# Where convolution inputs, third sums and a third split stand in four hand-written orders

## The chip, the cores and the metric

The kernel runs on one core of one Trainium2 chip. The metric is the device time of one execution in microseconds (us). Besides its five engines the core has 16 DMA engines; SP issues most transfers, ACT issues the gate tables.

## The reference, cut to what matters

Two layers follow one another, both on x of shape 32 x 64 x 1024. A layer has a convolution-like step and a feed-forward step whose result is added to x:

```python
# layer 0
y = conv1d(x, weight, taps=9, groups=4) + cond @ c_weight.T + bias       # 64 channels
x = x + y @ W.T + b + lora(y)                                            # W: 1024 x 1024, rank 16
# layer 1
mix_w, mix_b = softmax(mlp(cond)) @ (8 matrices, 8 biases)               # per sample
v = mix_w[sample] @ x + mix_b[sample]                                    # 64 x 64 over channels
scores = v @ Wr.T;  gates = softmax over the top 16 of 64 experts
h = v @ A.T          # 64 experts x rank 16 = 1024 columns
x = x + 2 * ((h * gates spread over 16 columns each) @ B)
```

All is f32. The kernel splits every operand of the large products in two parts, a high one (rounded to the matmul's type fp32r) and the rest as a low one, and makes three matmuls of each: high by high, high by low, low by high.

## The kernel before, in words

The 32 samples run as four groups of eight (512 tokens, four tiles of 128). Each group does, on PE: the convolution (`conv`, eight samples, banks shared with the end of the group before), the first product with W, the mixing (`mix`, eight column chunks), scores and h = v A (`h_of`, eight pieces), and the last product with B. Weights come in *pieces* of 128 x 1024. A raw piece lands in one of two (in the first group three) raw buffers, ACT writes its high part (`split_raw` or `split_first` on ACT), DVE its low part (the same names on DVE). The first group (`first_group` of every engine) uses 24 raw pieces plainly, piece 16 to 23 for the last product. The groups 1 to 3 (`group`) have 36 steps and use Strassen-Winograd for the two large products, seven half-size products instead of eight; a piece then takes 12 matmuls of 128 x 512 and not 24. The combined weights for that are made once: four *units* of four matrices are loaded (`load_weights`), summed on DVE (`combine`: four instructions), split (`combined_hi` on ACT, `combined_lo` on DVE) and written to DRAM (`keep_weights` on SP), from where later groups fetch them (`fetch`). Units 0, 1 and 2 fall in the first group, unit 3 in group 1. Units 1 to 3 use the buffer `conv_in` as their place of work, so that the next group's convolution inputs (`load_conv_in`, four loads of 516 KB) can only follow them.

Every engine's order is written out by hand, and only semaphores tie the engines. What the rest speaks of:

- SP's queue is in order: an instruction that waits holds up all that is behind it. `next_raw(n)` waits until DVE has made the low part of the piece two raw loads before (`lo_done`), then loads a raw piece. `next_x` waits until a tile pair of x has been stored and loads the next group's. `cond_bias` and `mix_bias` load bias tables of 256 KB.
- In the first group DVE multiplies h by the gates chunk by chunk (`gated`, `gated_lo`) and has `combine(2)` after chunk 5. The last product's piece 19 needs chunks 6 and 7 and `split_first(19)`.
- At the end of the first group DVE adds four half tiles (`add(banks[4 + t]...)`, then `dve.sem_inc(s_o, 8)`) to x. The convolution of group 1 takes those banks from its third sample on (`pe.wait_ge(s_o, g * 22 - 8)`). Just before these adds DVE makes the low parts of three raw pieces of group 1, `split_raw(0, STEPS + 0, 1, 2)`; SP loads the third of them by `next_raw(26)`.
- The gates go from `gate` through PE (transposed), ACT (`gates_out`) and DRAM to `gate_x`: eight loads of 256 KB (`spread_gates`), four after ACT's split of piece 20, four more as the buffers come free. DVE's `gated(g, c)` waits for the c-th. The last product needs all eight chunks from piece 24 on; after chunk 7 DVE makes four sums (`sums(4)`, L1162 to L1167) and then the low part of piece 25.

The lines that are printed below are those of the profile.

Of the kernel before, what the change touches and what calls it, by code (L numbers as in the profile page):

```python
# [69 lines left out]
def adaln_ffn_kernel(nc, conv_x, x, taps, pieces, first_consts, hidden_w, later_consts, lora_a, lora_b,  # L70
                     starts, wr, expand, spread, out):
    with ExitStack() as ctx:
# [240 lines left out]
        def _(sp):  # L313
# [82 lines left out]
            def first_group():  # L396
# [61 lines left out]
                load_conv_in(1, 3)  # L458
                for t in range(NT):
                    store(0, t, 0, t + 1)  # L460
                next_x(0, 0, 0)
                next_x(0, 1, 0)
                next_raw(26)
                next_raw(27)
                for t in range(NT):
                    store(0, t, 1, 11 + t)
                next_x(0, 0, 1)
# [4 lines left out]
            def group(g, last):  # L472
# [21 lines left out]
                next_raw(16)  # L494
                next_raw(17)
                if g == 1:
                    keep_weights(3, 0)
                    keep_weights(3, 1)
                next_raw(18)
                next_raw(19)  # L500
                if g == 1:
                    keep_weights(3, 2)
                    keep_weights(3, 3)
                for n in range(20, 24):
                    next_raw(n)
                    if not last:
                        load_conv_in(g + 1, n - 20)
                if not last:
                    cond_bias(g)
                    mix_bias(g)  # L510
                if g == 1:
                    for i in range(4):
                        sp.wait_ge(s_comb[i], 32 * 4)
# [111 lines left out]
        def _(act):  # L625
# [184 lines left out]
            def group(g, last):  # L810
                def next_split(n):

                    step_used(act, g, n - SLOTS)
                    split_raw(g, n)

                for b in range(GB):
                    conv_hi(g, b)
                    if b == 1:

                        act.wait_ge(s_conv, g * GB + 1)  # L820
                        split_raw(g, 3)
                first_product(g, 0, (4, 5))
                sums_hi(g, 0)
                lora_parts(g)
                next_split(8)
                next_split(9)
                next_split(14)
                next_split(15)
                for i, c in enumerate(CHUNKS):
                    split_hi(g, MIX0 + i, v_hi[:, c, :], work[:, c, :])  # L830
                if g == 1:
                    combined_hi(3, 0)
                    combined_hi(3, 1)
                score_out(g, 5)
                if g == 1:
                    combined_hi(3, 2)
                    combined_hi(3, 3)
                next_split(16)
                gates_exp(g)
                next_split(17)  # L840
                next_split(18)
                gates_out(g, 0)
                next_split(19)
                next_split(20)
                act.wait_ge(s_gates_out, 16 * g + 16)
                for c in range(GATES):
                    spread_gates(c)
                next_split(21)
                for c in range(NCH):
                    if g == 1 and c % 2 == 0:  # L850
                        act.wait_ge(s_comb[c // 2], 32 * 4)
                    gated_hi(g, c)
                    if c == 1:
                        next_split(22)
                    if c == 3:
                        next_split(23)
                    if c == 6:
                        next_split(24)
                next_split(25)
                first_product(g, 1, (6, 7))  # L860
                sums_hi(g, 4)
                next_split(32)
                next_split(33)
                if not last:
                    next_split(STEPS)
                    next_split(STEPS + 1)
                    next_split(STEPS + 2)
# [6 lines left out]
        def _(dve):  # L874
# [128 lines left out]
            def first_group():  # L1003
# [124 lines left out]
                for c in range(NCH):  # L1128
# [3 lines left out]
                    gated_lo(0, c)  # L1132
                    if c in (1, 3, 5):
                        split_first(16 + c // 2)
                    if c == 5:
                        combine(2)
                split_first(19)
                for step in range(4):
                    combined_lo(2, step)
                for n in range(20, 23):  # L1140
# [4 lines left out]
                dve.wait_ge(s_o, 4)  # L1145
                dve.sem_inc(s_o, 6)
                split_first(23)
                for n in range(3):
                    split_raw(0, STEPS + n)
                for t in range(NT):  # L1150
                    dve.wait_ge(s_fin, NT + t + 1)
                    add(banks[4 + t][:, :], t, 1, s_o)
                dve.wait_ge(s_o, 14)
                dve.sem_inc(s_o, 8)  # L1154
                for i in range(4):
                    dve.wait_ge(s_comb[i], 32 * 3)

            def group(g, last):
# [102 lines left out]
                for i, c in enumerate(CHUNKS):  # L1261
                    mix_item(g, i, c, (6, 7, 4)[i % 3])
                    if i:
                        mix_lo(g, i - 1, CHUNKS[i - 1])
                mix_lo(g, NCH - 1, CHUNKS[-1])
                if g == 1:
                    combined_lo(3, 0)
                    combined_lo(3, 1)
                split_raw(g, 16)
                choose(g, 1)  # L1270
                split_raw(g, 17)
                if g == 1:
                    combined_lo(3, 2)
                split_raw(g, 18)
                if g == 1:
                    combined_lo(3, 3)
                for n in range(19, 22):
                    split_raw(g, n)
                dve.wait_ge(s_lo, g * ITEMS + H0)
                for c in range(0, 6, 2):  # L1280
# [496 lines left out]
```

## Time and profile before

| | us |
|---|---|
| median of 3 runs | 690.73 |
| lowest, highest | 690.48, 694.65 |
| the profiled execution | 691.47 |
| its span, first to last instruction | 689.7 |
| PE busy in it | 659.3 (96%) |
| DVE, ACT, POOL busy | 453.2 (66%), 212.8 (31%), 74.4 (11%) |
| mean granted TensorE clock | 0.985 of full |
| traffic | 157.98 MB, 229 GB/s |

The profiled execution's time is 1.8 us more than its span. PE works nearly all the time, and matmuls are pipelined, so its busy share alone does not tell what can be had: one has to look at the places where it stands still and at the clock that it is granted. In a timeline row the bracket is the idle time of that engine before the instruction and what ended it. A row whose line is in a helper (L1355 to L1357 are the three matmuls of every product, L881 every `split_raw` of DVE, L887 every `split_lo`) has to be told apart by its time and its tiles.

### The profile page before, as it was taken

The numbers are of one execution on the slowest core, as the hardware profiler recorded it, in microseconds if no ns is written. First come the engines' busy times: TensorE is split into PE (matmuls) and PEld (weight loads), VectorE is DVE, ScalarE is ACT, GpSimd is POOL, SyncE is SP. The second block draws the span as 40 slices with busy tenths as digits, with TensorE's granted clock in tenths as the row PEclk, the third lists the DMA queues.
The fourth block names the chain that finished last, engine by engine and source line by source line (L and its number), as shares of the span: only waits on it lengthen the run. The fifth ranks groups of instructions, "written<-read, shape, count | busy, mean of one in ns | idle before, by whom it ended". The sixth has DMA issues, their size and how long they took to land.

```text
span 689.7 us, 8350 instructions
## 1 busy us (share of the span) xinstructions
PE 659.3 (96%) x3197; PEld 543.7 (79%) x3197; DVE 453.2 (66%) x688; ACT 212.8 (31%) x275; POOL 74.4 (11%) x91
## 2 busy tenths in 40 slices
PE   9999999989969999996999999999799999999997
PEld 8878888867868788875779788888588878888775
DVE  2869568557168786746768749644866965665864
ACT  2723234314133215224223402422513521243510
POOL 1699000000000070000000025000000000000000
PEclk9999999999989999998999999999999999999999
DMA  8568517948846852697785771077797666037585
GB/s 303 220 242 330 219 47 224 344 141 333 312 149 244 333 195 85 242 309 263 275 319 212 304 297 68 30 231 226 250 338 272 229 260 241 30 99 210 214 329 190
DMA packets 51450, 157.98 MB, mean 229 GB/s; under 512 B 5472, under 2 KB 6368, under 8 KB 51424
## 3 DMA queue, kind: packets, MB, share of 16 engines
q1 hardware_dynamic: 46096, 148.05, 59.4%
q10 hardware_dynamic: 5328, 9.61, 4.6%
q8 instruction: 13, 0.21, 0.1%
q14 instruction: 13, 0.11, 0.0%
HBM read 131.94 MB, written 25.71 MB: 229 GB/s over the span
## 4 chain that ended last, share of the span: by engine, by line
PE 43%; DMA 14%; DVE 8%; issue 3%; ACT 2%; SPq 1%; DVEq 0%; ACTq 0%
PE bank L1355 10%; PE bank L1357 10%; PE bank L1356 10%; DMA gate_x<-gates 7%; PE bank L1369 6%; DMA raw<-pieces 3%; DMA piece_lo<-kept 3%; PE bank L1389 3%; DVE piece_lo L881 2%; ACT piece_hi L634 1%; DVE work L976 1%; PE bank L1376 1%; DVE x L913 1%; PE bank L1395 1%; PE bank L1396 1%
## 5 line engine op out<-in xcount | busy, mean ns | idle before, releaser
L881 DVE TENSOR_TENSOR piece_lo<-raw,piece_hi 128x1024 fp32r<-128x1024 f32 x60 | 74.2, 1239 | 97.0 <-ACT piece_hi L634 97.0
L1355 PE MATMUL bank<-piece_hi,u_hi 128*128 128x512 f32 x272 | 110.8, 407 | 15.3 <-DVE u_lo L887 8.8
L634 ACT ACTIVATE piece_hi<-raw 128x1024 fp32r<-128x1024 f32 x60 | 63.2, 1056 | 161.0 <-PE bank L1357 109.0
L1357 PE MATMUL bank<-piece_hi,u_lo 128*128 128x512 f32 x272 | 109.9, 404 | 0.0
L1356 PE MATMUL bank<-piece_lo,u_hi 128*128 128x512 f32 x272 | 109.8, 404 | 0.0
L1355 PE MATMUL bank<-v_hi,piece_hi 128*128 128x512 f32 x256 | 101.9, 398 | 0.1
L1357 PE MATMUL bank<-v_hi,piece_lo 128*128 128x512 f32 x256 | 101.1, 395 | 0.0
L1356 PE MATMUL bank<-v_lo,piece_hi 128*128 128x512 f32 x256 | 101.0, 394 | 0.0
L1355 PEld LDWEIGHTS bank<-piece_hi,u_hi 128*128 128x128 f32 x272 | 52.5, 193 | 31.4 <-issue 10.6
L1355 PE MATMUL bank<-piece_hi,v_hi 128*128 128x512 f32 x192 | 76.2, 397 | 0.4 <-DMA piece_lo<-kept 0.3
L1357 PE MATMUL bank<-piece_hi,v_lo 128*128 128x512 f32 x192 | 75.8, 395 | 0.0
L1356 PE MATMUL bank<-piece_lo,v_hi 128*128 128x512 f32 x192 | 75.7, 395 | 0.0
L639 ACT ACTIVATE u_hi<-work 128x512 fp32r<-128x512 f32 x64 | 40.2, 631 | 112.9 <-DVE work L976 70.1
L1369 PE MATMUL bank<-toep,conv_in 128*128 128x128 f32 x512 | 61.9, 283 | 6.9 <-DVEq L1154 6.9
L1369 PEld LDWEIGHTS bank<-toep,conv_in 128*128 128x128 f32 x512 | 60.8, 199 | 7.7 <-DVEq L1154 7.1
L913 DVE TENSOR_TENSOR x<-x,bank 128x512 f32<-128x512 f32 x82 | 51.9, 680 | 19.1 <-PE bank L1383 12.7
L1357 PEld LDWEIGHTS bank<-piece_hi,u_lo 128*128 128x128 f32 x272 | 52.6, 193 | 12.5
L1356 PEld LDWEIGHTS bank<-piece_lo,u_hi 128*128 128x128 f32 x272 | 52.6, 194 | 11.9
L1355 PEld LDWEIGHTS bank<-v_hi,piece_hi 128*128 128x128 f32 x256 | 48.1, 188 | 11.6 <-DVE work L976 0.6
L1357 PEld LDWEIGHTS bank<-v_hi,piece_lo 128*128 128x128 f32 x256 | 48.1, 188 | 11.6
L1356 PEld LDWEIGHTS bank<-v_lo,piece_hi 128*128 128x128 f32 x256 | 48.2, 188 | 11.0
L887 DVE TENSOR_TENSOR u_lo<-work,u_hi 128x512 fp32r<-128x512 f32 x64 | 43.8, 687 | 15.1 <-ACT u_hi L639 13.5
(143 smaller groups left out, 802.8 us busy)
## 6 DMA issues: line engine op xcount, KB each, us to landing
raw<-pieces SPq DMA_DIRECT2D x76, 512.0 KB, 5.3
piece_hi<-kept SPq DMA_DIRECT2D x48, 512.0 KB, 4.7
piece_lo<-kept SPq DMA_DIRECT2D x48, 512.0 KB, 5.7
conv_in<-conv_x SPq DMA_DIRECT2D x16, 516.0 KB, 7.9
x<-x SPq DMA_DIRECT2D x16, 512.0 KB, 5.2
gate_x<-gates ACTq DMA_DIRECT2D x32, 256.0 KB
out<-x SPq DMA_DIRECT2D x32, 256.0 KB, 2.5
conv_in<-pieces SPq DMA_DIRECT2D x12, 512.0 KB, 8.3
```

The costliest lines, as they stand in the source:

```text
L634: act.activation(piece_hi[:, n % SLOTS, :], raw[:, r % RAWS, :], ACT.Copy).then_inc(s_piece_hi, 1)
L639: act.activation(to, of, ACT.Copy).then_inc(s_hi, 1)
L881: dve.tensor_tensor(piece_lo[:, n % SLOTS, :], raw[:, r % RAWS, :], piece_hi[:, n % SLOTS, :].bitcast(F32), ALU.subtract).then_inc(s_piece ...
L887: dve.tensor_tensor(to, of, hi, ALU.subtract).then_inc(s_lo, 1)
L913: dve.tensor_tensor(half, half, of, ALU.add).then_inc(done, 1)
L976: dve.tensor_tensor(work[:, c, :], banks[bank][:, :], gate_x[:, c % GATES, :], ALU.mult).then_inc(s_item, 1)
L1355: pe.matmul(to, left_hi, right_hi, start=first, stop=False)
L1356: pe.matmul(to, left_hi, right_lo, start=False, stop=False)
L1357: return pe.matmul(to, left_lo, right_hi, start=False, stop=last)
L1369: mm = pe.matmul(banks[bank][:, cg * P:(cg + 1) * P], conv_in[:, b, cg, h:h + Q], toep[:, cg, 1 - h, :], start=(h == 0), stop=(h == 1))
L1376: mm = pe.matmul(banks[bank][0:LORA_M, :], lora_a_r[:, k, :], part[:, k, :], start=(k == 0 and part is u_hi), stop=(k == NCH - 1 and part ...
L1389: mm = pe.matmul(banks[bank][:, t * P:(t + 1) * P], x1[:, t, c * P:(c + 1) * P], blockdiag[:, t, :], start=True, stop=True)
```

## The change

It only reorders; no operation is added or removed.

- SP, first group: `next_raw(26)` stands ahead of both `next_x`, `next_raw(27)` between them.
- SP, groups 1 to 3: the four `load_conv_in` of the next group no longer alternate with raw pieces 20 to 23. In group 2 two of them stand between raw pieces 17 and 18 and two behind 18; in group 1 all four stand behind 18, and all four `keep_weights(3, ...)` between 17 and 18. `cond_bias` and `mix_bias` stand ahead of raw pieces 22 and 23 and not behind them.
- ACT and DVE, group 1: the four `combined_hi(3, ...)` and `combined_lo(3, ...)` stand inside the mix loop, one for every two chunks, and not behind it and behind the choice of experts.
- DVE, first group: `combine(2)` stands behind `split_first(19)`; `split_raw(0, STEPS + 2)` behind the four adds to x.

```diff
--- before.py
+++ after.py
@@ -458,10 +458,10 @@
                 load_conv_in(1, 3)
                 for t in range(NT):
                     store(0, t, 0, t + 1)
+                next_raw(26)
                 next_x(0, 0, 0)
+                next_raw(27)
                 next_x(0, 1, 0)
-                next_raw(26)
-                next_raw(27)
                 for t in range(NT):
                     store(0, t, 1, 11 + t)
                 next_x(0, 0, 1)
@@ -494,20 +494,25 @@
                 next_raw(16)
                 next_raw(17)
                 if g == 1:
-                    keep_weights(3, 0)
-                    keep_weights(3, 1)
+                    for step in range(4):
+                        keep_weights(3, step)
+                elif not last:
+                    load_conv_in(g + 1, 0)
+                    load_conv_in(g + 1, 1)
                 next_raw(18)
-                next_raw(19)
                 if g == 1:
-                    keep_weights(3, 2)
-                    keep_weights(3, 3)
-                for n in range(20, 24):
+                    load_conv_in(g + 1, 0)
+                    load_conv_in(g + 1, 1)
+                if not last:
+                    load_conv_in(g + 1, 2)
+                    load_conv_in(g + 1, 3)
+                for n in range(19, 22):
                     next_raw(n)
-                    if not last:
-                        load_conv_in(g + 1, n - 20)
                 if not last:
                     cond_bias(g)
                     mix_bias(g)
+                next_raw(22)
+                next_raw(23)
                 if g == 1:
                     for i in range(4):
                         sp.wait_ge(s_comb[i], 32 * 4)
@@ -828,13 +833,9 @@
                 next_split(15)
                 for i, c in enumerate(CHUNKS):
                     split_hi(g, MIX0 + i, v_hi[:, c, :], work[:, c, :])
-                if g == 1:
-                    combined_hi(3, 0)
-                    combined_hi(3, 1)
+                    if g == 1 and i % 2 == 0:
+                        combined_hi(3, i // 2)
                 score_out(g, 5)
-                if g == 1:
-                    combined_hi(3, 2)
-                    combined_hi(3, 3)
                 next_split(16)
                 gates_exp(g)
                 next_split(17)
@@ -1132,9 +1133,8 @@
                     gated_lo(0, c)
                     if c in (1, 3, 5):
                         split_first(16 + c // 2)
-                    if c == 5:
-                        combine(2)
                 split_first(19)
+                combine(2)
                 for step in range(4):
                     combined_lo(2, step)
                 for n in range(20, 23):
@@ -1145,13 +1145,14 @@
                 dve.wait_ge(s_o, 4)
                 dve.sem_inc(s_o, 6)
                 split_first(23)
-                for n in range(3):
-                    split_raw(0, STEPS + n)
+                split_raw(0, STEPS)
+                split_raw(0, STEPS + 1)
                 for t in range(NT):
                     dve.wait_ge(s_fin, NT + t + 1)
                     add(banks[4 + t][:, :], t, 1, s_o)
                 dve.wait_ge(s_o, 14)
                 dve.sem_inc(s_o, 8)
+                split_raw(0, STEPS + 2)
                 for i in range(4):
                     dve.wait_ge(s_comb[i], 32 * 3)
 
@@ -1262,19 +1263,12 @@
                     mix_item(g, i, c, (6, 7, 4)[i % 3])
                     if i:
                         mix_lo(g, i - 1, CHUNKS[i - 1])
+                    if g == 1 and i % 2:
+                        combined_lo(3, i // 2)
                 mix_lo(g, NCH - 1, CHUNKS[-1])
-                if g == 1:
-                    combined_lo(3, 0)
-                    combined_lo(3, 1)
                 split_raw(g, 16)
                 choose(g, 1)
-                split_raw(g, 17)
-                if g == 1:
-                    combined_lo(3, 2)
-                split_raw(g, 18)
-                if g == 1:
-                    combined_lo(3, 3)
-                for n in range(19, 22):
+                for n in range(17, 22):
                     split_raw(g, n)
                 dve.wait_ge(s_lo, g * ITEMS + H0)
                 for c in range(0, 6, 2):
```

## Rows read from the trace of the kernel before

**Rows 1.** The page, part 1: busy time, share and count of each engine.

```profile
PE 659.3 (96%) x3197; PEld 543.7 (79%) x3197; DVE 453.2 (66%) x688; ACT 212.8 (31%) x275; POOL 74.4 (11%) x91
```

**Rows 2.** The waits of PE: who for whom, us in total, times, longest.

```profile
PE bank L1355 <- DVE u_lo L887: 8.8, 3, 3.6
...
PE bank L1355 <- DVE piece_lo L881: 2.8, 2, 1.5
```

**Rows 3.** Timeline of PE: start, us, instruction [idle before it <- releaser].

```profile
155.99 0.50 PE L1355 MATMUL bank<-piece_hi,u_hi 128*128 128x512 f32 x1 [3.50 <-DVE piece_lo L1053]
...
196.20 13.35 PE L1369 MATMUL bank<-toep,conv_in 128*128 128x128 f32 x96 [6.94 <-DVEq L1154]
...
316.03 0.49 PE L1355 MATMUL bank<-piece_hi,u_hi 128*128 128x512 f32 x1 [2.20 <-DVE u_lo L887]
...
326.44 0.49 PE L1355 MATMUL bank<-piece_hi,u_hi 128*128 128x512 f32 x1 [3.02 <-DVE u_lo L887]
...
332.41 0.51 PE L1355 MATMUL bank<-piece_hi,u_hi 128*128 128x512 f32 x1 [1.38 <-DVE piece_lo L881]
...
490.14 0.49 PE L1355 MATMUL bank<-piece_hi,u_hi 128*128 128x512 f32 x1 [3.61 <-DVE u_lo L887]
...
496.12 0.50 PE L1355 MATMUL bank<-piece_hi,u_hi 128*128 128x512 f32 x1 [1.47 <-DVE piece_lo L881]
```

**Rows 4.** Stretches: us, busy (count) per engine, clock, DMA share, GB/s.

```profile
156.80:160.20 3.40, 3.40 (x10) 2.63 (x9) 3.40 (x4) 3.40 (x4) 0.00 (x0) 0.50 0.95 353
194.40:201.20 6.80, 5.00 (x23) 5.00 (x24) 5.39 (x8) 2.10 (x3) 0.00 (x0) 0.50 0.82 269
332.40:486.00 153.60, 153.58 (x763) 128.00 (x764) 101.11 (x163) 42.77 (x57) 13.47 (x17) 1.00 0.63 221
```

**Rows 5.** The chain of work: start, us, a group's convolution undisturbed.

```profile
363.54 14.29 PE bank L1369 x128
```

**Rows 6.** Timeline of DVE before the first group's piece 20.

```profile
145.47 1.23 DVE L987 TENSOR_TENSOR conv_in<-conv_in 128x1024 f32<-128x1024 f32 x1 [6.26 <-DMA conv_in<-pieces]
...
154.71 1.23 DVE L1053 TENSOR_TENSOR piece_lo<-raw,piece_hi 128x1024 fp32r<-128x1024 f32 x1 [0.25 <-ACT piece_hi L741]
...
160.40 1.22 DVE L1053 TENSOR_TENSOR piece_lo<-partial,piece_hi 128x1024 fp32r<-128x1024 f32 x1
```

**Rows 7.** Timelines of SP, then DVE, around the group's end.

```profile
182.18 1.67 SPq L324 DMA_DIRECT2D x<-x  x2
183.90 0.94 SPq L315 DMA_DIRECT2D raw<-pieces  x2
...
192.53 1.23 DVE L881 TENSOR_TENSOR piece_lo<-raw,piece_hi 128x1024 fp32r<-128x1024 f32 x1 [12.09 <-ACT piece_hi L634]
193.68 2.47 DVE L913 TENSOR_TENSOR x<-x,bank 128x512 f32<-128x512 f32 x4
```

**Rows 8.** Stretches from first gate load's issue to last one's landing.

```profile
296.50:322.30 25.80, 23.45 (x93) 18.32 (x92) 13.52 (x18) 8.84 (x12) 0.00 (x0) 0.93 0.84 274
458.80:485.90 27.10, 27.10 (x118) 21.96 (x117) 13.01 (x18) 7.70 (x11) 0.00 (x0) 1.00 0.84 249
619.80:643.90 24.10, 24.10 (x105) 19.36 (x104) 14.44 (x20) 9.02 (x12) 0.00 (x0) 1.00 0.69 196
```

**Rows 9.** Timeline of SP in group 1: raw 18 with 19, cond bias.

```profile
277.48 7.68 SPq L315 DMA_DIRECT2D raw<-pieces  x2
...
302.55 0.43 SPq L353 DMA_DIRECT2D cond_bc<-spread  x1
```

**Rows 10.** Timeline of PE in the last group, inside pieces 24 and 25.

```profile
652.50 0.40 PE L1357 MATMUL bank<-piece_hi,u_lo 128*128 128x512 f32 x1
653.00 0.50 PE L1355 MATMUL bank<-piece_hi,u_hi 128*128 128x512 f32 x1
```

**Rows 11.** Groups of DVE in group 1's mix loop: line, shapes, count, busy, mean.

```profile
L887 DVE TENSOR_TENSOR v_lo<-work,v_hi 128x512 fp32r<-128x512 f32 x8 | 5.5, 684 | 0.2
L920 DVE TENSOR_TENSOR work<-bank,mixb_bc 128x512 f32<-128x512 f32 x8 | 5.4, 686 | 2.4 <-PE bank L1389 2.3
```


## The prediction

> **What bounds the kernel now.** I read the page's busy shares first: PE is busy 659.3 of 689.7 us [rows 1]. So the time is PE's work plus the places where it stands still or runs at the lower clock, and a reordering can only take from those. The waits of PE name them in total [rows 2]: it waits for `u_lo` three times (8.8 us) and twice for `piece_lo` L881 (2.8 us). The timeline of PE gives each wait's place [rows 3]. There are seven of weight:
>
> - A, first group, before piece 19: 3.50 us.
> - B, group 1's convolution, before its third sample: 6.94 us, until DVE has passed the adds at L1154.
> - C, group 1, around the last product: 2.20, 3.02 and 1.38 us, 6.6 together.
> - D, group 2, same place: 3.61 and 1.47 us, 5.1 together.
>
> Then the granted clock. It is 1.00 (2.4 GHz) nearly everywhere, but 0.50 (1.2 GHz) for 3.4 us after wait A and for 6.8 us around wait B [rows 4]. The same happened after the waits of 2.20, 3.02 and 3.61 us, three more stretches like the first row of [rows 4]. After the wait of 1.38 us it stayed at 1.00 [rows 3, 4]. So a wait of 1.5 us costs only itself and one of 2.2 us costs 3.4/2 = 1.7 us more. For B: 96 convolution matmuls took 13.35 us [rows 3]; undisturbed, 128 take 14.29 us [rows 5], so 96 take 10.7, and the loss is 2.6 us.
>
> What can be had at most is A 3.5 + 1.7 = 5.2, B 6.9 + 2.6 = 9.5, C 6.6 + 2 x 1.7 = 10.0, D 5.1 + 1.7 = 6.8; together 31.5 us.
>
> **Part A: `combine(2)` behind the split of piece 19.** DVE stood 6.26 us until the four matrices of unit 2 had landed, at 145.47, and then needed four sums of about 1.2 us, 4.8 us, before it came to chunks 6 and 7. The low part of piece 19 began at 154.71, ended at 155.94, and PE started at 155.99 [rows 3, 6]. Now the chunks come first. Piece 19's raw load is the next in the queue behind those matrices: 512 KB at the 353 GB/s of [rows 4] is 1.5 us, so it lands at about 147; ACT's and DVE's parts take 1.1 and 1.2, and the piece is ready at about 149. PE wants it at 155.99 - 3.50 = 152.4: wait A goes. The stall moves to piece 20. A whole piece is 24 matmuls, at 24.1/105 = 0.23 us each [rows 8] 5.5 us, so PE wants piece 20 at 157.9. DVE has four sums (4.8), four `combined_lo` (155.94 to 160.40, 4.5) and the split (1.2) before it: 149.2 + 10.5 = 159.7 [rows 6]. A wait of 1.8 us is left. From below it is 0, from above 3.5; I take 1.8, without a fall of the clock, which lies between the 1.47 that had none and the 2.20 that had one (plus 1.7 if it falls). A gives 5.2 - 1.8 = 3.4 us. Behind piece 20 DVE needs 1.2 us a piece against PE's 5.5, so nothing more is late.
>
> **Part B: `next_raw(26)` early, its split behind the adds.** SP issued the two x loads at 182.18, when the output stores had landed, and raw 26 at 183.90. DVE's low part of it began at 192.53 after 12.09 us idle, and only then came the four adds (2.47 us) for which PE waited [rows 7]. Now the adds need only PE's own results: they are done about 1 us after PE's last product, and the first two samples of the convolution, 2 x 14.29/8 = 3.6 us [rows 5], cover that. Wait B goes with its clock loss, 9.5 us. What is queued behind on DVE is the split of raw 26 and then `conv_item(0)`, which PE's fifth sample needs, 7.1 us after the convolution's start. That start was 196.20 - 6.94 - 3.6 = 185.7 and is now 3.4 earlier, 182.3, so the item is wanted by 189.4. Raw 26 can be issued once the low part of raw 24 is made, and DVE's idle time shows that this was before 180.4; taking 179 and the 7.5 us that it took last time (183.90 to 192.53 less ACT's 1.1) [rows 7] it lands at 186.5, is split by 188.8, and the item is there at 189.5. So it is hidden, narrowly; from above it costs some 3 us. The x loads are read only after the whole convolution, over 14 us later, so moving two of them behind one raw load costs nothing; without that cover it would be 1.5 us each. ACT waits for raw 26 ahead of `conv_hi` as before.
>
> **Parts C and D: conv loads out of the gates' stretch.** When could the last product start? In group 1 at once, 316.03 - 2.20 = 313.8; in group 2 two pieces of 12 matmuls ahead of its wait, 490.14 - 3.61 - 24 x 0.23 = 481.0; in group 3 three ahead, 652.7 - 36 x 0.23 = 644.4 [rows 3, 10]. The first gate load was issued at 296.5, 458.8, 619.8 and the last landed 25.8, 27.1, 24.1 us later [rows 8]. So the gates left 17.3, 22.2 and 24.6 us ahead of the product, and group 3, which loads no convolution input and no bias, waits 0.3 us in all [rows 10]. With the conv loads gone (group 2) and the keep stores of unit 3 gone from between raw 18 and 20 (group 1), ACT gets raw 20 as early as in group 3, and the gates leave as early. What group 3 does not have are two bias loads, now ahead of raw 22 [rows 9]: 512 KB, 1.5 us at 353 GB/s. From below they cost 0 (the DMA engines of group 3's stretch are busy 0.69), from above what a gate load takes there, 2 x 24.1/8 = 6 us. I take 1.5: a wait of 0.3 + 1.5 = 1.8 us stays in each of both groups. D gives 6.8 - 1.8 = 5.0 us.
>
> The conv loads themselves go where the queue is quiet: 4 x 516 KB is 6 us. In group 1 they stand behind raw 18 and ahead of raw 19, whose issue waits for DVE's choice of experts: the two issues lay 7.68 us apart [rows 9], and that hides them. Without that cover, raw 19 would be late by up to 6 us.
>
> C has a cost of its own: four `combined_lo` of 1.2 us inside the mix loop. DVE's own work there is 5.5 + 5.4 us with 2.4 us of waiting for PE [rows 11]. So the 4.9 us added exceed the idle time by 2.5, the upper bound; the lower is 0. The last one stands directly ahead of the low part of chunk 7, which PE needs; I take that one, 1.2 us. Two of them previously stood behind the loop and ahead of piece 16, so nothing else grows. C gives 10.0 - 1.8 - 1.2 = 7.0 us.
>
> **Sum.** 3.4 + 9.5 + 7.0 + 5.0 = 24.9 us. The profiled execution took 691.5 us (span 689.7 and 1.8 around it), which gives 666.6; the median of the runs is 0.7 lower, which would give 665.8. I say 666.
>
> **A rule that speaks against it.** In group 3's stretch without conv loads, the gate loads are only 1.7 to 3.0 us faster, at a DMA share of 0.69 against 0.84 [rows 8]. The Trainium skill (DMA: Bandwidth & Descriptors, Queues, rings and completion order) says that each DMA engine takes turns between the queues that have work for it, packet by packet. By it the gates on ACT's queue gain nothing as long as SP's queue still has raw pieces; then C and D would yield only what the earlier start gives. This is the first rival.
>
> **The rivals.**
>
> 1. *The gates are no earlier.* Raw pieces and biases keep SP's queue full, the waits of C and D stay as they are, and the mix loop costs its 1.2. Gain 3.4 + 9.5 - 1.2 = 11.7: 679.8 us. For it: 1.7 to 3.0 us of [rows 8]. Against it: group 3 waits only 0.3 us. Chance 0.17.
> 2. *Raw 26 lands late anyway.* Its landing is behind the group's conv loads and stores, PE stands at its fifth sample, and B gives about 3 of 9.5: 673 us. Against it: 7 us of cover. Chance 0.08.
> 3. *The other side: the clock.* PE without pauses is granted less for long stretches. All of PE's some 650 us scale with it, so each hundredth costs 6.5 us; from a mean clock of about 0.95 on, the end is later than before, at 0.94 near 698 us. Against it: 1.00 over 153.6 us of unbroken work [rows 4]. Chance 0.03.
>
> **Chances and range.** The forecast has 0.72, its own range is 660 to 672: from nearly all 31.5 us gained to 1.7 of clock lost again at piece 20 and in groups 1 and 2. The range of 8 in 10 reaches to just short of rival 1, 659 to 678. A change of 1% (7 us) is about what a measurement can tell. Faster by over 1% holds for the forecast and for both first rivals: 0.94; within 1%, if two rivals meet: 0.04; slower: 0.02.
>
> **What would show it.** In the profile after: no idle time before piece 19 and under 2.2 us before piece 20; no wait at L1154; the gate loads issued some 24 us before the last product in all of groups 1 to 3; waits below 2 us there and no clock of 0.50 behind them; 1 to 2 us new idle time before L1395/L1396 in group 1. Wrong would be: gate loads that leave early and land as late as before (rival 1), or PE idle inside the convolution of group 1 (rival 2).

## The result and the profile after

| | before | after |
|---|---|---|
| median of the runs, us | 692.65 (4 runs) | 671.66 (4 runs) |
| lowest, highest | 690.48, 694.65 | 669.35, 672.66 |
| profiled execution, span | 691.47, 689.7 | 671.31, 669.5 |
| PE busy | 659.3 | 651.7 |
| mean granted clock | 0.985 | 0.996 |

The ratio is 0.9693, with a 95% interval of 0.9646 to 0.974: the changed kernel is 3.1% faster, some 21 us. The forecast was 666 in a range of 659 to 678. In three further sets of runs, below, the kernel before was at 690.6, 691.0 and 691.7, and the changed kernel, in the last of them, at 671.1.

The page of the kernel after, part 1, to be laid beside [rows 1]:

```profile
PE 651.7 (97%) x3197; PEld 538.4 (80%) x3197; DVE 451.1 (67%) x688; ACT 213.1 (32%) x275; POOL 73.2 (11%) x91
```

PE has 7.6 us less busy time though it has the same 3197 matmuls: that is the clock, not work. The waits of PE after (who for whom, us in total, times, longest), beside [rows 2]:

```profile
PE bank L1349 <- DVE piece_lo L882: 4.6, 3, 2.4
PE bank L1349 <- DVE piece_lo L1054: 3.4, 1, 3.4
PE bank L1349 <- DMA piece_lo<-kept: 1.3, 2, 0.9
```

The 8.8 us for `u_lo` are gone altogether. What is left at L1349 is for low parts of pieces. Where they are, the timeline of PE after shows (seven waits, beside those of [rows 3]; the second row is group 1's convolution, the fourth and fifth are in its mix loop):

```profile
161.79 0.50 PE L1349 MATMUL bank<-piece_hi,u_hi 128*128 128x512 f32 x1 [3.37 <-DVE piece_lo L1054]
...
185.77 14.46 PE L1363 MATMUL bank<-toep,conv_in 128*128 128x128 f32 x128
...
221.60 0.50 PE L1349 MATMUL bank<-piece_hi,v_hi 128*128 128x512 f32 x1 [0.94 <-DMA piece_lo<-kept]
...
251.76 0.47 PE L1389 MATMUL bank<-v_hi,wr_r 128*128 128x512 f32 x1 [0.25 <-DVE v_lo L888]
...
254.35 0.50 PE L1389 MATMUL bank<-v_hi,wr_r 128*128 128x512 f32 x1 [0.30 <-DVE v_lo L888]
...
315.29 0.50 PE L1349 MATMUL bank<-piece_hi,u_hi 128*128 128x512 f32 x1 [1.04 <-DVE piece_lo L882]
...
474.81 0.51 PE L1349 MATMUL bank<-piece_hi,u_hi 128*128 128x512 f32 x1 [2.40 <-DVE piece_lo L882]
...
632.77 0.50 PE L1349 MATMUL bank<-piece_hi,u_hi 128*128 128x512 f32 x1 [1.16 <-DVE piece_lo L882]
```

The convolution of group 1 is now one unbroken row of 128 matmuls, where [rows 3] had 6.94 us of waiting. The waits of 2.20 and 3.02 us in group 1 and of 3.61 in group 2 have no answering row; one wait before piece 25 remains in each of groups 1 to 3 (1.04, 2.40, 1.16 us). But the first group's wait did not go: it moved from 155.99 to 161.79 and is 3.37 us instead of 3.50. The clock and the DMA engines in five stretches after (us, busy and count per engine, clock, DMA share, GB/s), beside [rows 4] and [rows 8]:

```profile
162.60:165.90 3.30, 3.30 (x9) 2.62 (x8) 3.30 (x6) 0.00 (x0) 0.00 (x0) 0.50 0.77 169
475.00:480.00 5.00, 5.00 (x22) 4.06 (x22) 5.00 (x7) 0.66 (x1) 0.00 (x0) 1.00 0.81 302
281.10:305.10 24.00, 24.00 (x105) 19.30 (x104) 13.52 (x19) 8.25 (x12) 0.00 (x0) 1.00 0.68 219
439.40:464.30 24.90, 24.90 (x109) 20.20 (x108) 13.50 (x18) 7.72 (x11) 0.00 (x0) 1.00 0.66 210
598.50:623.80 25.30, 25.30 (x110) 20.33 (x110) 14.73 (x20) 8.84 (x12) 0.00 (x0) 1.00 0.69 187
```

The clock fell to 0.50 once, behind the wait of 3.37 us, and not behind the one of 2.40. The three lower rows run from the first gate load's issue to the last one's landing: 24.0, 24.9 and 25.3 us in groups 1 to 3, where it was 25.8, 27.1 and 24.1 before [rows 8]. So the gates travel only 1.8 and 2.2 us faster in groups 1 and 2, and 1.2 us slower in group 3, where nothing was edited. The rest is when they leave. ACT's first gate loads and PE's first matmul of the last product, in groups 1 and 2:

```profile
281.11 2.89 ACTq L691 DMA_DIRECT2D gate_x<-gates  x4
...
439.44 2.56 ACTq L691 DMA_DIRECT2D gate_x<-gates  x4
```

```profile
305.68 0.40 PE L1349 MATMUL bank<-piece_hi,u_hi 128*128 128x512 f32 x1
...
463.88 0.39 PE L1349 MATMUL bank<-piece_hi,u_hi 128*128 128x512 f32 x1
```

The gates leave 24.6 and 24.4 us ahead of the product, where they left 17.3 and 22.2 us ahead before; group 3 has 24.5, as it had. In group 1 the earlier issue, 7.3 us, is most of what changed; in group 2 it is half, 2.2 us.

### The profile page after: what moved, and what is told of

Read it like the earlier page. It is cut to its first block, busy times and chain, and to the rows that moved or that the text cites. A ratio compares the mean times of both kernels' runs of the same rounds, so it can differ in the third digit from the quotient of the medians.

```text
span 669.5 us, 8350 instructions
## 1 busy us (share of the span) xinstructions
PE 651.7 (97%) x3197; PEld 538.4 (80%) x3197; DVE 451.1 (67%) x688; ACT 213.1 (32%) x275; POOL 73.2 (11%) x91
## 4 chain that ended last, share of the span: by engine, by line
PE 59%; DMA 19%; DVE 14%; issue 3%; ACT 3%; ACTq 1%; SPq 0%; DVEq 0%
PE bank L1349 14%; PE bank L1351 13%; PE bank L1350 13%; DMA gate_x<-gates 12%; PE bank L1363 8%; DMA piece_lo<-kept 4%; PE bank L1383 3%; DMA raw<-pieces 3%; DVE piece_lo L882 2%; PE bank L1370 2%; ACT piece_hi L639 2%; DVE work L977 1%; DVE x L914 1%; DMA toep<-taps 1%; PE bank L1375 1%
## 5 line engine op out<-in xcount | busy, mean ns | idle before, releaser
L1349 PE MATMUL bank<-piece_hi,u_hi 128*128 128x512 f32 x272 | 109.0, 401 | 8.1 <-DVE piece_lo L882 4.6
L1350 PE MATMUL bank<-piece_lo,u_hi 128*128 128x512 f32 x272 | 107.9, 397 | 0.0
L1351 PE MATMUL bank<-piece_hi,u_lo 128*128 128x512 f32 x272 | 107.8, 396 | 0.0
L1349 PE MATMUL bank<-v_hi,piece_hi 128*128 128x512 f32 x256 | 101.8, 398 | 0.0
L1349 PE MATMUL bank<-piece_hi,v_hi 128*128 128x512 f32 x192 | 76.2, 397 | 1.3 <-DMA piece_lo<-kept 1.3
L1349 PEld LDWEIGHTS bank<-piece_hi,u_hi 128*128 128x128 f32 x272 | 51.5, 189 | 22.1 <-DVE piece_lo L882 5.9
L1363 PE MATMUL bank<-toep,conv_in 128*128 128x128 f32 x512 | 59.5, 276 | 0.7 <-DMA toep<-taps 0.6
L1363 PEld LDWEIGHTS bank<-toep,conv_in 128*128 128x128 f32 x512 | 58.3, 192 | 1.6 <-DMA toep<-taps 1.1
L1349 PEld LDWEIGHTS bank<-v_hi,piece_hi 128*128 128x128 f32 x256 | 48.1, 188 | 11.0
```

The lines of the kernel that those rows point to most:

```text
L1349: pe.matmul(to, left_hi, right_hi, start=first, stop=False)
L1350: pe.matmul(to, left_hi, right_lo, start=False, stop=False)
L1351: return pe.matmul(to, left_lo, right_hi, start=False, stop=last)
L1363: mm = pe.matmul(banks[bank][:, cg * P:(cg + 1) * P], conv_in[:, b, cg, h:h + Q], toep[:, cg, 1 - h, :], start=(h == 0), stop=(h == 1))
```

## Experiments: which part gave what

Each ratio is to the kernel before, timed in the same set of runs.

**Part A alone.** On DVE, to the kernel before:

```diff
-                    if c == 5:
-                        combine(2)
                 split_first(19)
+                combine(2)
```

> The kernel before with part A alone: combine(2) stands behind the split of piece 19, on DVE. Theory 1 (the wait only moves): PE stands 3 to 4 us before piece 20 and not before piece 19, the clock falls behind it as before, and the time is that of before within 1 us. Theory 2 (the forecast's step): the wait before piece 20 is 1.8 us without a fall of the clock, and the time is about 3.4 us less than before.

Measured: 691.42 against 690.61 us, ratio 1.0012 (0.9984 to 1.0040), 12 runs of it. PE's timeline, before piece 20, and the stretch behind it:

```profile
160.76 0.50 PE L1354 MATMUL bank<-piece_hi,u_hi 128*128 128x512 f32 x1 [1.77 <-DVE piece_lo L1053]
```

```profile
162.10:165.40 3.30, 3.30 (x10) 2.52 (x9) 3.26 (x5) 0.00 (x0) 0.00 (x0) 0.50 0.73 217
```

The wait has moved to piece 20, as both theories said. It was 1.77 us, the size that the forecast had (1.8), not theory 1's 3 to 4; but the clock fell behind it, which makes 3.5 us of it, where wait A cost 5.2. The time is theory 1's all the same: in this profile the waits of group 1 are 9.3 us with one fall of the clock, where they were 6.6 us with two before, and those of group 2 are 5.4 instead of 5.1, so most of the remaining 1.7 us was lost there. Whether the edit did that or the execution, this run does not tell.

**The changed kernel without part A.** The same diff the other way round, on the changed kernel.

> The changed kernel with part A undone: combine(2) again behind chunk 5. Theory 1: the wait stands before piece 19 again, as long as the one before piece 20 was, and the time is that of the changed kernel within 1 us (0.97 of before). Theory 2: 3.4 us more than the changed kernel (0.974).

Measured: 669.60 us, ratio 0.9681 (0.9645 to 0.9717); the changed kernel has 0.9693 and 0.9673, in other sets. Part A gives nothing that can be measured. PE's wait before piece 19, and the stretch behind it:

```profile
155.50 0.50 PE L1350 MATMUL bank<-piece_hi,u_hi 128*128 128x512 f32 x1 [2.44 <-DVE piece_lo L1054]
```

```profile
155.60:162.00 6.40, 6.40 (x28) 5.04 (x29) 6.40 (x6) 5.22 (x6) 0.00 (x0) 1.00 0.85 322
```

This wait is longer than the one in the run before it, and the clock stayed at 1.00. The old order was seen in six profiles, with waits of 3.50, 1.94, 2.45, 2.44, about 2.0 and 3.5 us before piece 19; the new one in five, with 3.37, 3.00, 1.77, 2.0 and 1.17 before piece 20. These are profiles of different kernels that share the order at this place. The wait differs by 1.6 us among the old ones and by 2.2 us among the new ones; the means are 2.6 and 2.3 us, the clock fell behind it in four of six and in three of five, and so the two orders lie over each other.

**Part B alone.** On SP and on DVE, to the kernel before:

```diff
+                next_raw(26)
                 next_x(0, 0, 0)
+                next_raw(27)
                 next_x(0, 1, 0)
-                next_raw(26)
-                next_raw(27)
...
-                for n in range(3):
-                    split_raw(0, STEPS + n)
+                split_raw(0, STEPS)
+                split_raw(0, STEPS + 1)
                 for t in range(NT):
                     dve.wait_ge(s_fin, NT + t + 1)
                     add(banks[4 + t][:, :], t, 1, s_o)
                 dve.wait_ge(s_o, 14)
                 dve.sem_inc(s_o, 8)
+                split_raw(0, STEPS + 2)
```

> The kernel before with part B alone: next_raw(26) ahead of the two x loads, and the third split behind the four adds. The forecast's step: the wait of 6.9 us inside group 1's convolution goes, and the clock loss of 2.6 us with it; 9.5 us less than before. If B only moves its wait to the fifth sample, 3 us less.

Measured: 681.86 us, ratio 0.9868 (0.9836 to 0.9899), 9.1 us of 690.6. The waits of PE in it:

```profile
PE bank L1356 <- DVE u_lo L887: 9.3, 3, 4.9
PE bank L1356 <- DVE work L976: 2.3, 1, 2.3
...
PE bank L1356 <- DVE piece_lo L881: 1.2, 2, 0.7
```

The wait at L1154 is gone and nothing stands in its place inside the convolution. The waits of groups 1 and 2 are not those of [rows 2]: 9.3 + 2.3 + 1.2 us in the first, second and last row instead of 8.8 + 2.8, 1.2 us more, about a tenth of the gain. That was given back there, or was a chance of this execution.

**Half of part B: DVE's order only.**

> The kernel before with half of part B: the third split behind the four adds, SP's order as before. Raw 26 then lands at about 191 as before, conv_item(0) comes at about 194, and PE, whose third sample is now free, stands before its fifth sample (wanted at about 193): 1 to 2 us instead of 6.9, so 7 to 8 us less than before. If SP's order was what mattered, under 3 us less.

Measured: 684.13 us, ratio 0.9908 (0.9873 to 0.9942), 6.4 us less than before. **The other half, SP's order only.**

> The kernel before with the other half of part B: raw 26 ahead of the x loads, DVE's order as before. Raw 26 lands at about 186, is split by 188.5, and the adds follow until 190.5, where PE wants its third sample at about 189.5: 1 to 2 us of waiting instead of 6.9, so 7 to 8 us less than before. If DVE's order was what mattered, under 3 us less.

Measured: 683.23 us, ratio 0.9894 (0.9864 to 0.9924), 7.3 us less. The rows of PE that started behind the wait, first with DVE's order, then with SP's:

```profile
193.12 0.71 PE L1370 MATMUL bank<-toep,conv_in 128*128 128x128 f32 x4 [3.29 <-DVE work L891]
```

```profile
190.96 0.49 PE L1369 MATMUL bank<-toep,conv_in 128*128 128x128 f32 x2 [1.72 <-DVEq L1154]
```

With DVE's order alone the wait is at the fifth sample and for `work` L891, `conv_item(0)`, which stands behind the split of a raw piece that landed at 190.1; it is 3.29 us where 1 to 2 were expected. With SP's alone it is at the third sample, for the adds, and 1.72 us. Either half takes most of the wait, since both shorten the same chain (stores, x loads, raw 26, its split, adds); in the profiles only both take all of it. The times alone do not tell a half from the whole: their intervals, 4.0 to 8.8 and 5.2 to 9.4 us, overlap that of part B (7.0 to 11.3). Both halves were expected to give 7 to 8 us, which lies in both. In the changed kernel the tail of that chain runs on DVE as follows (last add, split of raw 26, first item of the convolution):

```profile
185.97 0.69 DVE L914 TENSOR_TENSOR x<-x,bank 128x512 f32<-128x512 f32 x1 [0.71 <-PE bank L1351]
186.80 1.23 DVE L882 TENSOR_TENSOR piece_lo<-raw,piece_hi 128x1024 fp32r<-128x1024 f32 x1
187.94 0.68 DVE L892 TENSOR_TENSOR work<-bank,cond_bc 128x512 f32<-128x512 f32 x1
```

The item starts at 187.94, 2.2 us after the convolution, and is wanted after 7.1.

**Parts C and D alone.** The changed kernel with parts A and B undone as in the two diffs above.

> The kernel before with parts C and D alone (everything that the change does in groups 1 to 3). The forecast's step: 12.0 us less than before (7.0 in group 1, 5.0 in group 2). What the profile after shows at its waits makes it 8 to 13. The rival of the gates that are no earlier: 1 us more than before.

Measured: 681.28 us, ratio 0.9851 (0.9817 to 0.9885), 10.3 us less; 12.0 had been forecast, and the first rival's +1 is excluded. Its waits of PE:

```profile
PE bank L1363 <- DVEq L1155: 6.3, 1, 6.3
PE bank L1349 <- DVE piece_lo L882: 4.8, 3, 2.3
```

The first row is wait B, which this kernel keeps. The second holds the three waits before piece 25, 4.8 us together with nothing for `u_lo`. No run takes part C apart: the keep stores, the convolution loads and the four `combined_lo` moved together in group 1, so which of them lets the gates leave 7 us earlier there is not shown.

**The changed kernel without part D.** On SP; group 1 keeps its order, in group 2 the convolution loads alternate with raw pieces 20 to 23 again and the bias loads follow them:

```diff
                     for step in range(4):
                         keep_weights(3, step)
-                elif not last:
-                    load_conv_in(g + 1, 0)
-                    load_conv_in(g + 1, 1)
                 next_raw(18)
                 if g == 1:
-                    load_conv_in(g + 1, 0)
-                    load_conv_in(g + 1, 1)
-                if not last:
-                    load_conv_in(g + 1, 2)
-                    load_conv_in(g + 1, 3)
-                for n in range(19, 22):
+                    for t in range(4):
+                        load_conv_in(g + 1, t)
+                next_raw(19)
+                for n in range(20, 24):
+                    if n == 22 and g == 1:
+                        cond_bias(g)
+                        mix_bias(g)
                     next_raw(n)
-                if not last:
+                    if g == 2:
+                        load_conv_in(g + 1, n - 20)
+                if g == 2:
                     cond_bias(g)
                     mix_bias(g)
-                next_raw(22)
-                next_raw(23)
```

> The changed kernel with part D undone: in group 2 the four convolution loads alternate with raw 20 to 23 again and the bias loads follow them. The forecast's step: the gates leave 2.4 us later and land later, PE waits 5 us more in group 2 and the clock may fall: 4 to 5 us more than the changed kernel. If SP's queue was full anyway, nothing changes.

Measured: 674.38 us, ratio 0.9763 (0.9719 to 0.9808); the changed kernel in the same set had 0.9673 (0.9628 to 0.9718). The difference of the ratios, 0.9 points or 6 us, is that of the forecast (5.0) within the intervals; that of the medians is 3.3 us. PE's two waits in group 2 of it:

```profile
470.42 0.49 PE L1347 MATMUL bank<-piece_hi,u_hi 128*128 128x512 f32 x1 [3.03 <-DVE u_lo L886]
...
476.40 0.79 PE L1347 MATMUL bank<-piece_hi,u_hi 128*128 128x512 f32 x1 [2.91 <-DVE piece_lo L880]
```

2.40 us after (2.91 in the other profile of the changed kernel) have become 3.03 + 2.91, with a clock of 0.50 behind the second. The gates left at 439.82 and the product began at 461.66, 21.8 us later instead of 24.4. So the place of the loads is the cause in group 2. The edit moves the bias loads too, but to behind raw 22, which can only help it (see below); that leaves the convolution loads.

**The changed kernel once more.**

> The changed kernel once more, unchanged, as the measure for the other three on the same chip: 0.967 to 0.970 of before. It also shows how much the waits behind gate loads vary from one execution to the next; if they are set by the order alone they are those of the profile after within 0.3 us.

Measured: 671.09 us, 0.9673 (0.9628 to 0.9718). The second expectation failed: the waits before piece 20, and before piece 25 in groups 1 and 2, were 3.00, about 1.7 and 2.9 us, against 3.37, 1.04 and 2.40; they differ by 0.4 to 0.7 us with the same kernel.

## Experiments: what is left

**Piece 20 ahead of the sums.** In the changed kernel, ACT and DVE get the same move; this is DVE's:

```diff
                 split_first(19)
+                split_first(20)
                 combine(2)
                 for step in range(4):
                     combined_lo(2, step)
-                for n in range(20, 23):
+                for n in range(21, 23):
                     split_first(n)
```

> The changed kernel with one more move: ACT and DVE make the parts of piece 20 before unit 2's sums. If the sums and combined_lo ahead of piece 20 (9.3 us of DVE) are what PE waits for, its wait there (3.4 us and a clock of 0.50 after it in the profile after) goes without another in its place, since piece 21 is wanted 5.5 us later: 2 to 5 us less than the changed kernel, about 0.965 of before. If piece 20's raw load or the gates are what is late, the wait stays and the time is that of the changed kernel.

Measured: 666.43 us, ratio 0.9653 (0.9622 to 0.9685). DVE's timeline, the splits of pieces 19 and 20 and the first sum:

```profile
149.70 1.23 DVE L1055 TENSOR_TENSOR piece_lo<-raw,piece_hi 128x1024 fp32r<-128x1024 f32 x1 [0.26 <-ACT piece_hi L746]
150.85 1.22 DVE L1055 TENSOR_TENSOR piece_lo<-partial,piece_hi 128x1024 fp32r<-128x1024 f32 x1
151.98 1.22 DVE L989 TENSOR_TENSOR conv_in<-conv_in 128x1024 f32<-128x1024 f32 x1
```

Piece 20 is ready at 152.1, six us before PE wants it; no wait is left in the first group's last product, and the granted clock was 1.00 from there to the end of group 2's waits. The wait is set by the nine DVE operations, not by a load. The time is 0.2 to 0.4 points, 1.4 to 2.8 us, below the changed kernel's two ratios, and the intervals overlap: that the wait is gone is shown, what it gives is not. And a new wait appeared. PE began the convolution at 180.52 here, 5.2 us earlier than after, and raw 26 was no longer in time for it:

```profile
188.03 3.84 PE L1365 MATMUL bank<-toep,conv_in 128*128 128x128 f32 x32 [0.21 <-DVE work L893]
192.32 3.84 PE L1365 MATMUL bank<-toep,conv_in 128*128 128x128 f32 x32 [0.44 <-DVE work L893]
```

**Bias loads ahead of raw 19.** In the changed kernel, on SP:

```diff
                 if not last:
                     load_conv_in(g + 1, 2)
                     load_conv_in(g + 1, 3)
+                    cond_bias(g)
+                    mix_bias(g)
                 for n in range(19, 22):
                     next_raw(n)
-                if not last:
-                    cond_bias(g)
-                    mix_bias(g)
                 next_raw(22)
```

> The changed kernel with the two bias loads behind the convolution loads, ahead of raw 19, in groups 1 and 2, and not ahead of raw 22. The forecast's step (the bias loads cost 1.5 us in each group because raw 22 lands later): raw 22 lands some 3 us sooner after its issue (8 to 9 us instead of 11 to 12), PE's waits before piece 25 in groups 1 and 2 fall to that of group 3 (0.3 to 1.4 us), 1 to 3 us less than the changed kernel. If the gate loads themselves are the limit, nothing changes.

Measured: 670.19 us, ratio 0.9708 (0.9669 to 0.9746): no gain, where 1 to 3 us were expected. (The profiled execution, 665.45 us, is the fastest of the six.) PE's waits before piece 25 in groups 1 and 2:

```profile
312.62 0.50 PE L1348 MATMUL bank<-piece_hi,u_hi 128*128 128x512 f32 x1 [2.92 <-DVE piece_lo L881]
...
470.17 0.51 PE L1348 MATMUL bank<-piece_hi,u_hi 128*128 128x512 f32 x1 [0.67 <-DVE piece_lo L881]
```

Group 2 did what was expected: raw 22 landed 8.3 us after its issue instead of 11.8, and the wait is 0.67 instead of 2.40 us. With the bias loads ahead of raw 22 that wait was 2.30 to 2.91 us in all five profiles, and with them early, here and in the two runs below, 0.58 to 1.16 us. In group 1 it grew, from 1.04 to 2.92 us; there the order of the changed kernel gave 1.04 to 1.74 us in five profiles and 2.72 in the sixth (no_d). ACT's timeline in group 1 shows a likely cause (the split of raw 19, then the first gate load):

```profile
277.72 1.06 ACT L638 ACTIVATE piece_hi<-raw 128x1024 fp32r<-128x1024 f32 x1 [3.88 <-DMA raw<-pieces]
...
279.23 0.60 ACTq L690 DMA_DIRECT2D gate_x<-gates  x1
```

ACT had moved the gates out at 273.24 and then stood 3.88 us for raw 19; the first gate load left 6.0 us behind that, where it took 3.2 us after, and so 21.7 us ahead of the product instead of 24.6. Ahead of raw 19 stand six loads, 2.6 MB; with the four of 2.1 MB ACT stood 0.64 us for it after and 1.43 in no_d.

**Both, with the bias loads ahead of raw 18.** p20's diff, and on SP:

```diff
                 elif not last:
                     load_conv_in(g + 1, 0)
                     load_conv_in(g + 1, 1)
+                if not last:
+                    cond_bias(g)
+                    mix_bias(g)
                 next_raw(18)
...
-                if not last:
-                    cond_bias(g)
-                    mix_bias(g)
                 next_raw(22)
```

> The changed kernel with piece 20's split ahead of unit 2's sums (as in p20), and the two bias loads ahead of raw 18 and not of raw 19. Ahead of raw 19 they brought raw 20 in late in group 1 and so held the gates; ahead of raw 18 the queue is quiet. So: gates leave 3.5 us behind PE's transposition in group 1 as in the profile after, raw 22 lands some 8 us after its issue in groups 1 and 2, waits before piece 25 of at most 1.5 us in both: 1 to 3 us less than p20, 0.960 to 0.964 of before.

Measured: 667.35 us, ratio 0.9632 (0.9587 to 0.9678). In group 2 the wait was 0.58 us; in group 1 it was 2.92 again, since the gates' store and raw 20 still landed some 2 us later than after. That expectation failed for group 1. The ratio lies in the 0.960 to 0.964 that were expected, 1.4 us below p20's and inside its interval. **And unit 3's loads behind the fetches of pieces 6 and 7.**

```diff
+                fetch(g, 6)
+                fetch(g, 7)
                 if g == 1:
                     for i in range(4):
                         sp.wait_ge(s_comb_in[i], 48)
                         load_weights(3, i)
-                fetch(g, 6)
-                fetch(g, 7)
```

> best1 with the four loads of unit 3 behind the fetches of pieces 6 and 7, so that these do not queue behind 2 MB. PE's wait for a fetched piece at about 221 (1.1 us after, 0.3 before) goes; unit 3 lands some 2 us later, 10 us before DVE sums it. 0.3 to 1 us less than best1.

Measured: 665.98 us, ratio 0.9625 (0.9583 to 0.9666), the lowest of all. The wait for a fetched piece near 221, 0.94 us after, is not there. But it is under 0.2 us too in the second profile of the changed kernel and in no_a, cd_only, p20, bias_early and best1, which all have unit 3's loads ahead of the fetches, and it is 0.36 in no_d: this run does not show that the edit did anything. The time differs from that of best1 by less than either's interval. Against the changed kernel of the same set (0.9673, 671.09 us) it is 0.5 points, or 3 us, faster, and 5 us by the medians; the intervals overlap, so this is likely and not shown. Not tried: the bias loads early in group 2 and where the change has them in group 1, which the two profiles suggest.

## Why the prediction was right

The measured 671.66 lies in the range and some 5 us above the number. The sum was made for the profiled execution: 666.6, and that took 671.3. Step by step:

- **The reading of what bounds the kernel held.** PE's matmuls did not change, and all of the gain is in its waits and clock, as named.
- **A was the step that failed in size.** The forecast said 3.4 us: a wait of 1.8 without a clock loss in place of 3.5 with one. In the profile after the wait is 3.37 us and the clock fell, so that 0.1 is left of it, and a_only and no_a both say nothing within 2 us. The mechanism was right (the wait moves to piece 20, nine DVE operations ahead of it, as p20 shows). Two terms were off. The start of the chain was put at 149.2, when raw 19 would be ready; but chunk 7's gate load was later:

```profile
147.70 0.69 DVE L977 TENSOR_TENSOR work<-bank,gate_x 128x512 f32<-128x512 f32 x1 [1.86 <-DMA gate_x<-gates]
...
150.05 1.23 DVE L1054 TENSOR_TENSOR piece_lo<-raw,piece_hi 128x1024 fp32r<-128x1024 f32 x1 [0.26 <-ACT piece_hi L746]
151.19 1.22 DVE L988 TENSOR_TENSOR conv_in<-conv_in 128x1024 f32<-128x1024 f32 x1
...
155.98 4.62 DVE L1001 TENSOR_TENSOR v_lo<-conv_in,v_hi 128x1024 fp32r<-128x1024 f32 x4
160.52 1.22 DVE L1054 TENSOR_TENSOR piece_lo<-partial,piece_hi 128x1024 fp32r<-128x1024 f32 x1
```

  `gated(7)` waited for its gates until 147.70, so piece 19's low part ended at 151.2, the sums began there and piece 20's began at 160.52 and not 158.5. And the forecast took a clock without a fall for the smaller wait, where a_only shows one behind 1.77 us. [Rows 3, 4] had only one execution; over six profiles the old order's wait averages 2.6 us and not 3.5, so there was less to be had.
- **B was right**: 9.5 forecast, 9.1 (b_only, 7.0 to 11.3). Raw 26 was issued at 176.2, landed at about 185.5, one us earlier than forecast (186.5), and the convolution item behind its split began 5 us before it was wanted. That cover, narrow in the forecast, was wide by luck: as A gave nothing, PE began the convolution at 185.77 and not at 182.3. In p20, where it began at 180.52, the cover was gone and PE stood 0.65 us.
- **C and D were nearly right**: 12.0 forecast, 10.3 measured together (7.9 to 12.6), D alone 6 by no_d against 5.0. The step that carried them, gates that leave some 24 us ahead of the product, is there (24.6 and 24.4). The mix loop has the idle time that was named, before L1389 (L1395 in the code before): from its first score matmul to its last it takes 12.6 us where it took 11.8, 0.8 more against 1.2. (The 0.25 us at its first one stood there before too.) DVE's groups in that loop, beside [rows 11], show that its idle time was filled:

```profile
L921 DVE TENSOR_TENSOR work<-bank,mixb_bc 128x512 f32<-128x512 f32 x8 | 5.3, 678 | 0.0
L1001 DVE TENSOR_TENSOR u_lo<-conv_in,u_hi 128x1024 fp32r<-128x1024 f32 x4 | 4.9, 1216 | 0.3 <-ACT u_hi L703 0.3
```

  The 2.4 us of waiting for PE in [rows 11] are 0.0 now, and the four `combined_lo` take 4.9.
- **The bias loads cost about what the forecast said.** SP issued them ahead of raw 22, and DVE stood 4.11 us for it in group 2 (SP's, then DVE's timeline):

```profile
440.13 0.73 SPq L353 DMA_DIRECT2D cond_bc<-spread  x1
...
441.53 0.66 SPq L315 DMA_DIRECT2D raw<-pieces  x1
```

```profile
454.51 1.23 DVE L882 TENSOR_TENSOR piece_lo<-raw,piece_hi 128x1024 fp32r<-128x1024 f32 x1 [4.11 <-ACT piece_hi L639]
```

  The wait left is 2.40 us where 1.8 was forecast; bias_early takes 1.7 of it away in group 2, where the forecast had 1.5 for these loads. In group 1 the wait left is 1.04.
- **Not in the sum** were group 3, whose wait before piece 25 went from 0.3 to 1.16 us with no edit (from under 0.2 to 1.34 us in the other profiles), and the fetched pieces, 1.3 us instead of 0.3. Together 1.9 us, and most of it differs as much among profiles of one order.
- Over all, against the profiled execution: A 3.3 less than forecast, D 0.6 less, group 3 and the fetches 1.9 less, C 1.1 more: 4.7 us, the whole gap. That it fits to a tenth is chance; smaller differences, as 0.7 us in the start of the first product (24.97 and not 24.26), are not in it.
- **The rivals.** The gates that are no earlier: refuted by cd_only and no_d. Half of its ground held: once they had left, the gates landed only 1.8 and 2.2 us sooner, while the DMA share fell from 0.84 to 0.68 and 0.66. What it missed is the earlier start, 7.3 us in group 1 and 2.2 in group 2. Its rule (the Trainium skill, DMA: Bandwidth & Descriptors, Queues, rings and completion order) is that engines take turns between the queues that have work; no run here shows the turns themselves. A late raw 26: refuted by the unbroken convolution, with the luck named under B. The clock: refuted; the mean rose to 0.996, and in p20 it was 1.00 over 323 us from 152 on.

## What to carry to other kernels

When an engine waits behind a block of work on another, moving the block by one consumer only moves the wait: count what the block is in front of after the move, and put it where the next consumer is furthest away (here behind piece 20, not behind piece 19). A queue in order should have its large loads in front of an instruction that waits for something late anyway, and the room there is finite: in group 1 four loads of 0.5 MB fitted between raw 18 and 19, and with two of 0.25 MB more the gates left 3 us later. When a transfer is late, look at when it was issued before looking at how fast it went: here most of the gain in group 1 is an earlier issue. A wait read from one profile is one draw: the same wait differed by 0.4 to 0.7 us between two profiles of one kernel, and by 1.6 to 2.2 us among kernels that share the order around it.

## What the hardware did that I had not expected

The clock does not fall at a certain length of a wait. It fell to 0.50 for 3.4 us behind waits of 1.77 us (a_only) and 2.20 us (before), and stayed at 1.00 behind waits of 2.44 (no_a, above), 2.40 (after), 3.29 and 3.37 (b_dve) and 2.92 us:

```profile
312.70:320.00 7.30, 7.30 (x32) 5.94 (x33) 6.91 (x9) 0.77 (x1) 0.00 (x0) 1.00 0.85 332
```

This is the stretch behind bias_early's wait of 2.92 us in group 1. The same wait of 2.92 us in best1 and best2 was followed by 3.4 us at 0.50. The low stretch can be twice as long: the first row is around no_a's wait of 2.91 us in group 2, the second around b_only's of 2.58.

```profile
472.40:479.10 6.70, 6.14 (x15) 4.80 (x16) 5.19 (x8) 1.41 (x2) 0.00 (x0) 0.50 0.68 236
480.10:486.80 6.70, 5.66 (x13) 3.98 (x14) 6.60 (x7) 5.06 (x7) 0.00 (x0) 0.50 0.61 220
```

In the fourteen profiles no wait of up to 1.74 us between matmuls had the clock fall behind it, every one of 3.50 us or more had, and of those from 1.77 to 3.37 us some had and some had not. So a wait of that middle size costs itself, or 1.7 us more, or up to 3.4 us more, and which of these could not be told from these runs. That this makes a part of the spread of one kernel's times is likely: of the changed kernel's six runs in the last set the two fastest, 665.0 and 667.1 us, have mean clocks of 0.998 and 0.999, the four at 671.1 to 671.3 have 0.993 to 0.996. No run was made for it.
